# Where two leftover keys' values are added: moved from ScalarE and GpSimd to VectorE in a cross-attention and expert kernel

## The reference, cut to what matters

```python
x = x + xattn(ctx, ctx, layernorm(x))      # 4096 queries, 3202 keys, width 512
x = x + ffn(layernorm(x))                  # 16 experts, top 2, 512 places each

# xattn: kp = k Wk^T; vp = v Wv^T + bv; qp = q Wq^T + bq
#        softmax(qp kp^T / sqrt(512)) vp Wo^T + bo
```

## Time and profile before

| | us |
|---|---|
| runs before | 1742.08, 1739.48, 1741.78 (median 1741.78) |
| the profiled execution's own time | 1741.16 |
| its span, first to last instruction | 1739.4 |
| PE busy | 1606.2 (92%) |
| DVE busy | 1164.9 (67%) |
| POOL busy | 873.4 (50%) |
| ACT busy | 719.1 (41%) |
| POOL line 820 (the additions of `v_rel`) | 105.9 in 64 instructions, mean 1655 ns |
| ACT line 931 (the products `v_rel`) | 42.7 in 64 instructions, mean 714 ns |

### The profile page before, as it was taken

The page is one execution under the profiler, slowest core; times in us unless marked ns, Lnnn a source line. Parts: engine busy times, 40 slices in busy tenths (PEclk is TensorE's granted clock), DMA queues, the critical chain, the costliest instruction groups (busy, mean ns, idle before and its releaser), DMA issues. The chain is left out here.

```text
span 1739.4 us, 41578 instructions
## 1 busy us (share of the span) xinstructions
PE 1606.2 (92%) x15821; PEld 1062.4 (61%) x15821; DVE 1164.9 (67%) x2271; ACT 719.1 (41%) x1060; POOL 873.4 (50%) x832
## 2 busy tenths in 40 slices
PE   8999989999999999999999999999997389999964
PEld 4444768666776677766777667766674144545530
DVE  4443276788777887778877888778786365555524
ACT  2443244444444444444444444444443134545440
POOL 0100064566555665566655666556665346565540
PEclk9999999999999999999999999999998689999985
DMA  4310111122111221212111121111210069899869
GB/s 157 92 43 13 50 32 44 44 47 49 44 45 43 48 48 44 51 38 56 46 44 45 44 51 45 44 45 44 50 38 25 26 196 207 216 209 215 187 96 377
DMA packets 202315, 140.93 MB, mean 81 GB/s; under 512 B 135010, under 2 KB 151394, under 8 KB 202148
## 3 DMA queue, kind: packets, MB, share of 16 engines
q1 hardware_dynamic: 179696, 94.27, 19.7%
q0 software_dynamic: 16896, 35.42, 10.6%
q10 hardware_dynamic: 5556, 8.66, 1.3%
HBM read 86.65 MB, written 51.68 MB: 80 GB/s over the span
## 5 line engine op out<-in xcount | busy, mean ns | idle before, releaser
L47 PE MATMUL sc<-qt,kT 128*128 128x128 f16 x3100 | 523.1, 219 | 12.7 <-issue 12.7
L45 PE MATMUL sc<-qt,kT 128*128 128x128 f16 x3100 | 523.1, 219 | 10.3 <-DMA qt<-blocks_q 6.7
L46 PE MATMUL sc<-qt,kT 128*128 128x128 f16 x3100 | 523.0, 219 | 0.0
L45 PEld LDWEIGHTS sc<-qt,kT 128*128 128x128 f16 x3100 | 303.2, 98 | 19.0 <-issue 13.1
L47 PEld LDWEIGHTS sc<-qt,kT 128*128 128x128 f16 x3100 | 303.2, 98 | 14.9 <-issue 14.9
L45 PE MATMUL acc<-vv,pT 128*128 128x512 f16 x800 | 305.0, 381 | 4.4 <-DVE pT L1047 4.4
L46 PE MATMUL acc<-vv,pT 128*128 128x512 f16 x800 | 305.2, 381 | 0.0
L47 PE MATMUL acc<-vv,pT 128*128 128x512 f16 x800 | 305.0, 381 | 0.0
L46 PEld LDWEIGHTS sc<-qt,kT 128*128 128x128 f16 x3100 | 303.3, 98 | 2.0
L856 POOL TENSOR_TENSOR sum<-sum,s_T 128x512 f32<-128x512 f32 (+1 forms) x160 | 281.6, 1760 | 26.4 <-ACT s_T L907 5.9
L896 ACT ACTIVATE s_T<-sc 128x512 f32<-128x512 f32 (+1 forms) x224 | 120.0, 548 | 301.4 <-PE sc L47 297.6
(11 more groups left out here) (296 smaller groups left out, 2916.5 us busy)
## 6 DMA issues: line engine op xcount, KB each, us to landing
xq<-in_x_dram SPq DMA_DIRECT2D x32, 256.0 KB, 2.7
x_in<-in_x_dram SPq DMA_DIRECT2D x32, 256.0 KB, 3.2
raw_g<-in_L_ffn_w_gate_dram SPq DMA_DIRECT2D x16, 512.0 KB
raw_f<-in_L_ffn_w_fc_dram SPq DMA_DIRECT2D x16, 512.0 KB
raw_p<-in_L_ffn_w_proj_dram SPq DMA_DIRECT2D x16, 512.0 KB
y_dram<-x SPq DMA_DIRECT2D x32, 256.0 KB, 2.0
rows_dram<-row SPq DMA_DIRECT2D x32, 256.0 KB, 2.0
y_sb<-y_dram SPq DMA_DIRECT2D x16, 512.0 KB, 16.0
```

The costliest lines, as they stand in the source:

```text
L45: pe.matmul(out, s_hi, m_hi, start=first, stop=False)
L46: pe.matmul(out, s_hi, m_lo, start=False, stop=False)
L47: return pe.matmul(out, s_lo, m_hi, start=False, stop=last)
```

## The change

The two products and additions are made by DVE with two instructions, each `x1 = v_tail[i] * p_rel[i] + (xb or x1)`, between the three subtractions of tile t+1 and its three lower halves. `xb` is then `x_in + bo_row` alone. ACT's `tail_values`, the buffer `v_rel` and the semaphore `vr_rdy` are gone. `residual` adds `x1` in place of `xb`. The waits for `xb_rdy`, for the store of the x1 before and for ACT's last reading of it stand in front of the two instructions, and no longer in `residual`. A `drain` makes DVE wait for its own writes.

```diff
                 def add_bias(t):
...
-                    pool.tensor_tensor(xb[:], x_in[:], bo_row[:], ALU.add)
-                    for i in range(TAIL):
-                        pool.drain()
-                        pool.wait_ge(vr_rdy, TAIL * t + i + 1)
-                        added = pool.tensor_tensor(xb[:], xb[:], v_rel[:, i, :], ALU.add)
-                    added.then_inc(xb_rdy, 1)
+                    pool.tensor_tensor(xb[:], x_in[:], bo_row[:], ALU.add).then_inc(xb_rdy, 1)
...
-                def tail_values(t):
-                    act.wait_ge(rinv_rdy, t + 1)
-                    wait_for(act, xb_rdy, t)
-                    for i in range(TAIL):
-                        act.activation(v_rel[:, i, :], v_tail[:, i, :], ACT.Copy, scale=p_rel[:, i:i + 1]).then_inc(vr_rdy, 1)
...
-                    wait_for(dve, vr_rdy, TAIL * t)
                     dve.tensor_scalar(p_rel[:], p_tail[:], rinv[:], None, ALU.mult).then_inc(rinv_rdy, 1)
...
+                def tails(t):
+
+                    dve.drain()
+                    dve.wait_ge(xb_rdy, t + 1)
+                    wait_for(dve, x1_out, 16 * t)
+                    wait_for(dve, xs_rdy, t)
+                    for i in range(TAIL):
+                        dve.scalar_tensor_tensor(out=x1[:], in0=v_tail[:, i, :], scalar=p_rel[:, i:i + 1],
+                                                 in1=x1[:] if i else xb[:], op0=ALU.mult, op1=ALU.add)
+                        dve.drain()
+
                 def residual(t):
 
                     dve.wait_ge(pv_part, NG * (t + 1))
-                    dve.wait_ge(xb_rdy, t + 1)
-                    wait_for(dve, x1_out, 16 * t)
-                    wait_for(dve, xs_rdy, t)
-                    dve.scalar_tensor_tensor(out=x1[:], in0=acc[:], scalar=rinv[:], in1=xb[:],
+                    dve.scalar_tensor_tensor(out=x1[:], in0=acc[:], scalar=rinv[:], in1=x1[:],
                                              op0=ALU.mult, op1=ALU.add).then_inc(x1_rdy, 1)
...
                     inverse(t)
                     if more:
                         shift(t + 1, 1 - h, more_q)
+                    tails(t)
                     if not more:
                         route(t - 1)
                     for g in range(NG if more else 0):
...
                 inverse(0)
                 shift(1, 1, True)
+                tails(0)
                 for g in range(NG):
                     low(1, 1, g)
```

More of the change, by code:

```diff
@@ L635, in attend @@
         p_rel = buf("p_rel", [P, TAIL], F32)
-        v_rel = buf("v_rel", [P, TAIL, D], F32)
         neg_mean = buf("neg_mean", [P, 1], F32)
@@ L702, in attend @@
         qb_rdy, qb_out = sem("qb_rdy"), sem("qb_out")
-        rinv_rdy, vr_rdy = sem("rinv_rdy"), sem("vr_rdy")
+        rinv_rdy = sem("rinv_rdy")
         x_ld = sem("x_ld")
@@ L962, in step @@
                         rows_high(t - 1)
-                        tail_values(t)
-                    if more:
-                        tail_values(t)
                     if post:
@@ L1059, in inverse @@
                     dve.drain()
-                    wait_for(dve, vr_rdy, TAIL * t)
                     dve.tensor_scalar(p_rel[:], p_tail[:], rinv[:], None, ALU.mult).then_inc(rinv_rdy, 1)
-                def residual(t):
-                    dve.wait_ge(pv_part, NG * (t + 1))
+                def tails(t):
+                    dve.drain()
                     dve.wait_ge(xb_rdy, t + 1)
@@ L1068, in residual @@
                     wait_for(dve, xs_rdy, t)
-                    dve.scalar_tensor_tensor(out=x1[:], in0=acc[:], scalar=rinv[:], in1=xb[:],
+                    for i in range(TAIL):
+                        dve.scalar_tensor_tensor(out=x1[:], in0=v_tail[:, i, :], scalar=p_rel[:, i:i + 1],
+                                                 in1=x1[:] if i else xb[:], op0=ALU.mult, op1=ALU.add)
+                        dve.drain()
+                def residual(t):
+                    dve.wait_ge(pv_part, NG * (t + 1))
+                    dve.scalar_tensor_tensor(out=x1[:], in0=acc[:], scalar=rinv[:], in1=x1[:],
                                              op0=ALU.mult, op1=ALU.add).then_inc(x1_rdy, 1)
```

## The result

The changed kernel takes 1754.85 us (median of 1758.08, 1751.71, 1751.81 and 1757.88) against 1741.65 (a fourth run of the kernel before, 1741.52, is in this median), a ratio of 1.0085, interval 1.007 to 1.010; the two medians alone give 1.0076. The forecast of 1739.9 had the wrong sign. The time lies inside the outer range of 1727 to 1759, but not in the forecast's own of 1733 to 1747. Rival 1 (1762), which had been given a chance of 0.15, named what happened.

The account below looks back on a forecast made before the run. PE, the fullest engine, was seen waiting for DVE's `diag`, the back edge and the query-tile DMA, with little DVE slack. A lap of 72.06 against 72.15 gave -1.3 over 14 laps, 1741.16 to 1739.9; range 1733 to 1747, outer 1727 to 1759.

Parts of the forecast that it names:

- Rival 1: `diag` stays held in the back-edge step: step 37.69 us, lap +1.47, total 1762; chance 0.15.
- ACT and POOL work removed: 0: Two products fewer on ACT and two additions fewer on POOL per step, off PE's path: by itself 0.
- Subtractions 5.79 to 3.64: DVE's three subtractions no longer wait for the second addition of line 820: gain of 2.15 us a step.
- Tails 1.73 each, with turns: DVE's two new instructions: 0.66 us own time plus 1.07 for a turn with POOL's sum, 3.46 for both.
- VectorE's delay d = 1.31: Net delay of DVE per step: 3.46 for the tail instructions less 2.15 gained at the subtractions, 1.31 us.
- Plain step 35.93: Loop step without back edge: 35.93 us against 34.99, PE waiting about 0.9 us at `greatest`.
- Step with the back edge 36.13: `diag` takes the port first, `spread` does not wait (-0.64), DMA wait 0.13 for 0.52: 36.13 us against 37.16.
- R: The end of line 1028 on DVE; 706.79 in step 13 and 743.29 in step 14.
- G: The start of `greatest` on PE; 707.28 in step 13 and 744.10 in step 14.
- Rival 3: The additions of line 820, removed by the change, were what held `diag`: 1728; chance 0.07.
- Rival 2: The tail instructions on DVE take no turns with POOL's sums, or short ones: 1727 or 1737; chance 0.13.
- rival 4: A bigger delay of DVE, near 1.8 us: plain step 36.4, lap 72.6, total 1748; chance 0.15.

Follow-up runs that it names:

- Experiment 5: Kernel before plus two otherwise useless statistics of `bo_row` on VectorE behind the lower halves, ahead of `residual`: 1756.40 us, ratio 1.0078.
- 9: Changed kernel with `diag` on ScalarE and GpSimd's x_in + bo_row ahead of the scatter: 1723.96 us, ratio 0.9887.
- 12: Kernel before with `diag` on ScalarE and GpSimd's x_in + bo_row ahead of the scatter: 1724.85 us, ratio 0.9898.
- experiment 2: Changed kernel with the two tail instructions 8 columns wide and `residual` reading `xb`: 1740.79 us, ratio 0.9970.
- Experiment 3: Changed kernel with GpSimd's addition x_in + bo_row put ahead of the scatter: 1728.56 us, ratio 0.9900.
- 6: Changed kernel with one drain on GpSimd between the two indirect DMAs and the addition x_in + bo_row: 1741.39 us, ratio 0.9998.
- 8: Kernel before with x_in + bo_row ahead of the scatter, the two `v_rel` additions left behind it: 1722.52 us, ratio 0.9879.
- experiment 11: Kernel before with one drain on GpSimd between the indirect DMAs and its first addition: 1727.66 us, ratio 0.9921.

## Why the prediction was wrong, point by point

- **ACT and POOL work removed: 0.** Nothing speaks against it. Experiment 5 gives the loss with that work in place, and 9 and 12 are alike.
- **Subtractions 5.79 to 3.64.** Measured 3.63. Right.
- **Tails 1.73 each, with turns.** Measured 1.48 and 1.61 as durations, 3.33 from the first's start to the lower halves' start. 3.33 for 3.46, right within 0.2 and for the reason given; experiment 2 shows the turn apart from the streaming. The lower halves took 6.60 for 6.85.
- **VectorE's delay d = 1.31.** Measured 1.19: 732.96 - 719.28 = 13.68 us against 723.46 - 710.97 = 12.49.
- **Plain step 35.93.** Measured 35.37 on average. The sum took the part from `residual` to line 1028 for rigid. It is not: it went from 18.64 us (759.97 to 778.61) to 18.19 (770.53 to 788.72). GpSimd's `mr_q`, on the way from the query tile's statistics to ScalarE, took 0.60 us before and 0.19 after, having come at another moment to VectorE's maximum; the next maximum, which waits for ACT, came some 0.3 sooner with it. The other 0.13 lie at `p_rel`, whose wait for `vr_rdy` the change took away. This error was in favour of the change: 0.56 a lap, 8 us over 14 laps.
- **Step with the back edge 36.13: the step that failed.** The text said that `diag` takes the port first, since it starts 0.79 after R and line 816 at 1.26. It does start ahead of it (715.77 and 716.36, with R at 714.97: 0.80 and 1.39 after R), and is held to the end of the addition nonetheless. In place of the gain of 0.64 before `spread` there is a loss of 0.50 (1.13 for 0.63), and the DMA's wait, which hangs on `diag` too, nearly stays (0.81 here, 0.43 on average for 0.52 before; 0.13 was forecast). The measured mean is 37.73 for 36.13, that is 1.60 a lap and 22 us over 14 laps. Less the 8 us of the plain steps this is 14 to 15 us, about the distance from the forecast to the measured median. Rival 1 had 37.69 by the right mechanism; that it comes so close is in part luck, since its DMA wait of 0.66 was too long and its 2.59 up to `spread` (2.75 measured) too short. Its 1762 is too high because it took over the 35.93.
- **Why it failed.** From step 13, where `diag` started 0.09 us early and lost, I concluded that 0.47 would do, since that is more than `diag` lasts. The rows did not bear that: they held lost races alone, and no `diag` that had won against an addition queued directly behind the DMAs. Experiment 3 rules out the DMAs as holders, 6, 8 and 11 show that `diag` passes in 0.3 to 0.5 us when a drain keeps the addition 1.5 us off. What holds `diag` therefore acts ahead of the addition's recorded start: early enough to catch a `diag` that starts 0.60 ahead and would have ended 0.3 ahead, and too late for the one that started 0.77 ahead. Whether the port is claimed that early or the recorded start is late is open; both fit all runs. It is not so ahead of every GpSimd instruction: in experiment 2 the second tail instruction started 0.27 us ahead of a sum that was not queued behind a DMA, and passed.
- **Rival 3** (the v_rel additions hold `diag`, so that their going frees it) fell as argued: they are gone and `diag` is held longer. **Rival 2** fell by the tails' durations, **rival 4** by d = 1.19.
- **Two slips in the text that no sum uses.** An unheld `diag` ends 1.17 us sooner after G and not 0.87; the wait of 0.13 is worked out with 1.17. And d without turns is -0.67 by a duration of 0.74, or -0.83 by 0.66, and not -0.6.

What the loss consists of, then: at the end of the plain step VectorE arrives some 0.75 us later against PE. The first 0.42 are slack. The rest, 0.33, makes the plain step longer: 0.18 as a wait at the transposition and 0.17 as PE's busy time, 34.83 for 34.66. In the step behind it `mx` follows R as closely as it can, while the addition's time is tied to VectorE's own chain, so that `diag` is held 0.5 us longer after `mx` (1.96 for 1.46). Together 0.38 + 0.58 = 0.96 us a lap.

## What to carry to other kernels

A chain on a second engine with half a microsecond of slack is on the path already: price an added instruction by what that chain arrives late, not by the engine's idle share (VectorE was 79% busy in the loop). Before moving work away from a wait, find out which instruction holds the waiting one, by comparing end times, and try first to move that holder: here one moved addition on GpSimd was worth 20 us, and the change under study, once that was done, nothing in the loop. That does not hold for every cure: with the drain, which puts the addition in among the subtractions, the change still cost 12 to 14 us. And where a forecast hangs on who comes first at a shared port, count it as lost unless the trace has a case that was won with no more of a head start.

## What the runs showed of the hardware that I had not expected

- A VectorE instruction in a position to pass was held by a GpSimd addition whose recorded start was 0.59 us later (0.46 in experiment 5), when the addition stood directly behind indirect DMAs. With a head start of 0.77 us it passed. Without an addition behind them the DMAs held it by 0.2 us at most (0.50 us in experiment 11, where a drain follows), and in experiment 3 not at all.
- A drain on GpSimd behind an indirect DMA comes with 1.5 us of idle time ahead of the next instruction (1.50, 1.45 and 1.49 in experiments 6, 8 and 11; 0.2 to 0.4 where it stands behind an addition), and that distance can be worth having.
- Two statistics of VectorE, which GpSimd's sums did not hold (1.27 us for both), were nearly free between instructions that take turns with the sums: they cost 0.10 us, because GpSimd used the time for a turn that it would have taken anyway. Behind the last of these instructions the same two cost 1.2 (experiment 5). A tail instruction of 8 columns took 0.96 beside a sum.
